# Four graph layers on one core: who writes the three parts of the weighted one-hots

## The chip, the cores and the metric

The kernel runs on one core of one Trainium2 chip. The metric is the device time of one execution in microseconds (us), lower is better. The engines are named as the profile names them: PE (TensorE; PEld its weight loads), DVE (VectorE), ACT (ScalarE), POOL (GpSimd) and SP, which only issues DMAs.

## What is computed

Four graph layers over N = 6250 nodes of 256 features and E = 106250 edges (100000 random ones, made symmetric, and a loop for each node), sorted by destination. Each layer is added to its input and normalized. Cut to what matters:

```
edge_index = stack([src, dst])
x = layernorm(x + L0(x))        # attention over rows of x picked by src and dst
x = layernorm(x + L1(x))        # out = segment_sum(h[src] * norm, dst),           h = x @ W
x = layernorm(x + L2(x))        # two GCN layers with edge weights and self loops:
                                #   out = segment_sum(dinv[row]*w*dinv[col] * h[row], col) + b, relu
x = layernorm(x + L3(x))        # out = segment_sum(vals * h[dst], src),           h = x @ W.T
```

So layers 1 and 2 (L2 holds two of them) sum the rows of a table h over the edges of each destination, and layer 3 sums over the edges the other way. The kernel calls the sum of layer 1 pass 1, the two of layer 2 passes 2 and 3, and the last one pass 4.

## The kernel before

The nodes are cut into NBK = 49 blocks of 128. The edges of a destination block fill NC = 18 chunks of 128 edges. In pass 1 a chunk is one gather of 128 rows (POOL, L2109, an indirect DMA into one of NG = 7 tiles G), a one-hot M of the destinations (DVE, L1287, NM = 4 tiles), and one matmul (PE, L2008) that adds M times the gathered rows to the block's sum. ACT writes the edge's weight into a last column of G (L1621).

Behind pass 1, in the same loop over its 882 chunks, runs the build of adjacency matrices for later passes. For the blocks of BORDER, one for every PITCH = 17 chunks, the edges are sorted into cells by pairs of blocks (cellhot, pick, pack, place on DVE; totals, rank, permute on PE; L1346 to L1380 and L1889 to L1907). Then ACT copies the cells' contents from PSUM, step "cells": the low part of the source ids to clf, everything in 16 bits to clb, and, for a dense block, the third part of the weights to clw in 32 bits (L1665 to L1668). A block has NPOS = 26 positions, two to a batch (CB = 2), so NBT = 13 batches. For each batch:

- DVE, step "pairhot": doh, one-hots of destinations, 128 x 256 in 16 bits (L1392), two of soh, one-hots of sources (L1394), and in a dense block the weighted one-hots wdoh, parts 0 and 1 (L1398).
- ACT, step "third": part 2 of wdoh, by one ACTIVATE for each of the two positions (L1676), with the weight as its scale. It waits for doh.
- PE, step "pair": doh times soh into PSUM (L1919). PE, step "weigh", dense blocks alone: soh times each of the three parts of wdoh, 6 matmuls for each position (L1931). It waits for wdoh of DVE (`s_v`) and of ACT (`s_tw`), and then for a free PSUM bank.
- ACT, steps "keep" and "keepw": the finished PSUM banks to atf or atp (L1685, L1688) and to awp (L1695). SP stores them from there (AT and AW).

A weight is the sum of three 16-bit parts, so that the matmuls in 16 bits give it in full. The last NDW = 22 blocks (numbers from NBW = 27 on) are dense: they have weighted matrices too, which passes 2 and 3 then load in place of gathers (L1967). BORDER spreads the 22 dense among the 27 sparse ones, so that mostly one follows the other. The tiles doh, soh and wdoh have NB = 4 buffers; DVE takes one again when PE's pairs and weighs of the batch four before are done. The PSUM banks of the build are a ring of three.

The order on each engine is fixed in the program. `build_steps` gives each step a due chunk: for a batch that starts at `at_`, pairhot at `at_`, third at `at_ + 1`, pair at `at_ + 1`, weigh at `at_ + 2`, keep at `at_ + 2`, keepw at `at_ + 3`, and 26 positions are spread over 17 chunks. An engine runs, for each chunk, first what the pass itself needs, then the steps that are due, in order, and waits where it has to. `chunks_of` is 882 for pass 1, 29 and 27 blocks' worth for passes 2 and 3.

Of the kernel before, what the change touches and what calls it, by code (L numbers as in the profile page):

```python
# [10 lines left out]
ALU = mybir.AluOpType  # L11
# [4 lines left out]
P = 128  # L16
# [16 lines left out]
CB, NB = 2, 4  # L33
# [600 lines left out]
def program(nc, a, out):  # L634
# [6 lines left out]
    with ExitStack() as ctx:  # L641
# [100 lines left out]
        slots = sb("slots", [P, NBK, NC])  # L742
        clb = [sb(f"clb{i}", [P, 5, NPOS], BF16) for i in range(2)]
        clf = [sb(f"clf{i}", [P, NPOS]) for i in range(2)]
        clw = [sb(f"clw{i}", [P, NPOS]) for i in range(2)]
        payw = sb("payw", [P, NDW, 3, NC], BF16)
        wrest = sb("wrest", [P, NDW, NC])
        cell = sb("cell", [P, NBK, NC], BF16)
# [185 lines left out]
        def vector(e):  # L934
# [3 lines left out]
            def done(ins, name=None):  # L938
                ins.then_inc(s_v, 1)
                n[0] += 1  # L940
                if name is not None:
                    at[name] = n[0]
                return n[0]
# [370 lines left out]
            def behind_(step):  # L1314
# [20 lines left out]
                elif kind == "cellhot":  # L1335
                    O_ = OH[j]
                    if i == 0:
                        w.wait_ge(s_ct, NPR + 2)
                        w.wait_ge(s_io, 7)
                        w.wait_ge(s_ev, project_of(1, NBK - 1) + 1)  # L1340
                        after("dsum", "d1")
                    if i >= 2:
                        w.wait_ge(s_rk, i - 1)
                        after(("load", i - 2))
                    w.wait_ge(s_du, i + 1)
                    done(e.tensor_tensor(twos(O_[:, :, :]), twos(celltab[:, own, :].unsqueeze(1).to_broadcast([P, NC, NPOS])),  # L1346
                                         celld[j][:, :, :].unsqueeze(2).to_broadcast([P, NC, NPOS // 2, 2]), ALU.is_equal), ("cellhot", i))
                elif kind == "pick":
                    w.wait_ge(s_rk, i + 1)
                    if i:  # L1350
                        after(("pack", i - 1))
                    done(e.tensor_tensor(sel[:, :, :], PR[:, 0:NPOS * NC].rearrange("p (c t) -> p c t", t=NPOS), OH[j][:, :, :],
                                         ALU.mult), ("pick", i))
                elif kind == "pack":
                    after(("pick", i))
                    if i:
                        after(("slots", i - 1))
                    done(e.tensor_reduce(slot0[:, :], sel[:, :, :], AX.X, ALU.add), ("pack", i))
                elif kind == "over":
                    after(("pack", i))  # L1360
                    done(e.scalar_tensor_tensor(out=OH[j][:, :, own + 1], in0=slot0[:, :], scalar=127.5, in1=OH[j][:, :, own],
                                                op0=ALU.is_ge, op1=ALU.mult), ("over", i))
                elif kind == "less":
                    after(("over", i))
                    done(e.tensor_tensor(OH[j][:, :, own], OH[j][:, :, own], OH[j][:, :, own + 1], ALU.subtract), ("less", i))
                elif kind == "slots":
                    done(e.scalar_tensor_tensor(out=slots[:, b, :], in0=OH[j][:, :, own + 1], scalar=-128.0, in1=slot0[:, :],
                                                op0=ALU.mult, op1=ALU.add), ("slots", i))
                elif kind == "load":
                    after(("less", i))  # L1370
                    w.wait_ge(s_pm, NC * i)
                    q_ = 5 if b >= NBW else 2
                    for q in range(q_):
                        done(e.tensor_tensor(twos(OHP[:, :, q, :]), payd[j][:, :, q, :].unsqueeze(2).to_broadcast([P, NC, NPOS // 2, 2]),
                                             twos(OH[j][:, :, :]), ALU.mult), ("load", i))
                elif kind == "place":
                    c = step[2]
                    after(("slots", i))
                    w.wait_ge(s_pm, NC * (i - 1) + c + 1)
                    done(e.tensor_scalar(S[:, c, :], iob[:, 0:P], slots[:, b, c:c + 1], None, ALU.is_equal), ("place", i, c))  # L1380
                elif kind == "pairhot":
                    n_ = NBT * i + step[2]
                    j0 = CB * step[2]
                    g = min(CB, NPOS - j0)
                    value = lambda q, m_: clb[j][:, q, j0:j0 + g].unsqueeze(1).to_broadcast([P, m_, g])
                    w.wait_ge(s_ce, i + 1)
                    if n_ >= NB:
                        before = n_ - NB
                        w.wait_ge(s_pc, batch_end(before))
                        if BORDER[before // NBT] >= NBW:  # L1390
                            w.wait_ge(s_wg, batch_end(before) - NPOS * (before // NBT - weighed_before(before // NBT)))
                    done(e.tensor_tensor(doh[n_ % NB][:, :, 0:g], irepD[:, :, 0:g], value(1, P), ALU.is_equal), ("doh", n_))  # L1392
                    for q in range(g):
                        done(e.tensor_scalar(soh[n_ % NB][:, q, :], iob[:, :], clf[j][:, j0 + q:j0 + q + 1], None, ALU.is_equal),  # L1394
                             ("pairhot", n_))
                    if b >= NBW:
                        after(("doh", n_))
                        done(e.tensor_tensor(wdoh[n_ % NB][:, 0:2, :, 0:g], doh[n_ % NB][:, :, 0:g].unsqueeze(1).to_broadcast([P, 2, P, g]),  # L1398
                                             clb[j][:, 2:4, j0:j0 + g].unsqueeze(2).to_broadcast([P, 2, P, g]), ALU.mult), ("weighted", n_))
                elif kind == "bad":  # L1400
                    after(("place", NBK - 1, NC - 1))
                    done(e.tensor_scalar(slots[:, :, :], slots[:, :, :], 127.5, 0.0, ALU.is_ge, ALU.add, accum_out=bad[:, :]), "bad")
                elif kind == "pad":

                    built(w)
                    w.wait_ge(s_bad, 1)
                    done(e.memset(keyS[96:128, ETAIL:EC], 8192), "pad")
                elif kind == "split":
                    w.wait_ge(L["src"], 3 * 16)
                    after("pad")  # L1410
                    done(e.tensor_scalar(tS[0][:, :], keyS[:, :], 7, None, ALU.logical_shift_right), "kS0")
                    done(e.tensor_scalar(tS[1][:, :], keyS[:, :], 127, None, ALU.bitwise_and), "kS1")
                    after("kS0")
                    done(e.tensor_copy(hi[:, :], tS[0][:, :]))
                    after("kS1")
                    done(e.tensor_copy(lof[:, :], tS[1][:, :]), "keysS")
                elif kind == "deg":
                    if b == 0:
                        w.wait_ge(s_io, 9)
                        after("keysS")  # L1420
                    if b < NDEG:
                        degrees(b)
                elif kind == "dinv" and b == 0:
                    w.wait_ge(s_dgs, NDEG)
                    done(e.tensor_scalar(degS[:, :], PR[:, 0:NBK], 1.0, None, ALU.add), "degS")
                elif kind == "dinv" and b == 1:
                    w.wait_ge(s_sq3, 1)
                    for i in range(4):
                        newton("d3n", i, d3[:, :], degS[:, :], [t_[:, :] for t_ in rs])
                    at["d3"] = at["d3n", 3]  # L1430
                else:
                    w.wait_ge(s_bad, 1)
                    done(e.tensor_scalar(ok[:, 1:2], PC[:, 0:1], 0.5, None, ALU.is_lt), "ok1")
                    after("ok1")
                    done(e.tensor_tensor(ok[:, 0:1], ok[:, 0:1], ok[:, 1:2], ALU.mult), "ok")
                    after("ok")
                    done(e.tensor_copy(flag[:, :], ok[0:1, 0:1]), "flag")
# [76 lines left out]
        def scalar(e):  # L1514
# [126 lines left out]
            def behind_(step):  # L1641
# [16 lines left out]
                elif step[0] == "cells":  # L1658
# [5 lines left out]
                        w.wait_ge(s_v, max(at["pairhot", n_], at.get(("weighted", n_), 0)))  # L1664
                    e.copy(clf[i % 2][:, :], PC[:, 0:NPOS])  # L1665
                    if q_ == 5:
                        e.copy(clw[i % 2][:, :], PC[:, 4 * NPOS:5 * NPOS])
                    e.copy(clb[i % 2][:, 0:q_, :].rearrange("p k t -> p (k t)"), PC[:, 0:q_ * NPOS]).then_inc(s_ce, 1)  # L1668
                elif step[0] == "third":

# [2 lines left out]
                    w.wait_ge(s_ce, i + 1)  # L1673
                    w.wait_ge(s_v, at["doh", n_])
                    for q in range(min(CB, NPOS - j0)):
                        ins = e.activation(wdoh[n_ % NB][:, 2, :, q], doh[n_ % NB][:, :, q], ACT.Copy, scale=clw[i % 2][:, j0 + q:j0 + q + 1])  # L1676
                    ins.then_inc(s_tw, 1)
                elif step[0] == "keep":
                    i, m_ = step[1], step[2]
# [614 lines left out]
```

## Time and profile before

| | us |
|---|---|
| median of 3 runs | 3351.84 |
| lowest and highest | 3343.08, 3353.5 |
| the profiled execution | 3345.05 |
| its span, first to last instruction | 3343.2 |
| PE, DVE, ACT, POOL busy | 3084.6, 2304.2, 1742.7, 2036.7 |
| mean granted clock of PE | 0.976 of full speed |

A busy time is the time in which the engine has at least one instruction running; matmuls overlap, and so do ACT's instructions where they follow each other closely. So counts times mean durations can be more than the busy time. An engine's share of the span is a mean over stages that have different limits; for a change that lies in one stage the windows of that stage are the view to read, cut by what its loop repeats.

### The profile page before, as it was taken

The page shows a single profiled execution, that of the slowest core. Times are in us where ns is not written, and L with a number is a line of the kernel's source. Part 1 is how long each engine was busy: PE and PEld are TensorE (multiplying, and loading weights), DVE is VectorE, ACT ScalarE, POOL GpSimd, SP SyncE. Part 2 cuts the span into 40 slices and gives each one's busy share as a digit, 9 for nine tenths or more (in the row PEclk, how much of TensorE's full clock was granted, in tenths as well). Part 3 has the DMA queues.
Part 4 walks back from the last instruction along what each step waited for, and adds up shares of the span by engine and source line. Part 5 has one row for each costly group of instructions (what it writes and reads, how often), then busy time and mean ns, then how long its engine had stood idle before and what let it go on. Part 6 is the DMA issues. An engine that isn't in the chain of part 4 may idle for free.

```text
span 3343.2 us, 58417 instructions
## 1 busy us (share of the span) xinstructions
PE 3084.6 (92%) x18262; PEld 2501.9 (75%) x18262; DVE 2304.2 (69%) x9060; ACT 1742.7 (52%) x4775; POOL 2036.7 (61%) x2042
## 2 busy tenths in 40 slices
PE   6788988989988989799999999799999998999999
PEld 5665667757766667578888888688888886888887
DVE  6657988998899889567777777566666664323333
ACT  3555767767767767534444444344444453323232
POOL 6627777777777777677777777577777771000000
PEclk9899999999999999999999999899999999999999
DMA  6246878878778878666666666776667666444443
GB/s 199 76 178 193 255 233 257 253 236 256 248 240 261 253 227 257 216 195 204 206 202 204 204 200 199 238 217 211 214 208 216 210 201 226 151 142 147 167 167 117
DMA packets 335271, 692.18 MB, mean 207 GB/s; under 512 B 63028, under 2 KB 180496, under 8 KB 334062
## 3 DMA queue, kind: packets, MB, share of 16 engines
q1 hardware_dynamic: 237134, 424.16, 37.5%
q0 software_dynamic: 95888, 262.38, 27.4%
q8 instruction: 151, 2.47, 0.3%
q10 hardware_dynamic: 1936, 1.84, 0.2%
q14 instruction: 162, 1.33, 0.1%
HBM read 497.33 MB, written 190.82 MB: 206 GB/s over the span
## 4 chain that ended last, share of the span: by engine, by line
PE 68%; DVE 16%; DMA 7%; POOL 3%; ACT 3%; issue 2%; SPq 0%; DVEq 0%; ACTq 0%
PE PS L1967 25%; PE PS L2039 15%; PE PS L2010 6%; PE PS L2008 6%; DMA G<-T,idx 5%; DVE soh L1394 4%; PE PS L1931 3%; PE PS L1790 3%; DVE M L1287 2%; PE PS L1791 2%; DVE S L1380 2%; PE PS L1948 2%; DVE doh L1392 2%; POOL G L2109 2%; PE PS L1919 2%
## 5 line engine op out<-in xcount | busy, mean ns | idle before, releaser
L2109 POOL DMA_INDIRECT G<-T,idx x1890 | 1913.8, 1013 | 643.3 <-issue 267.5
L1967 PE MATMUL PS<-H,aw 128*128 128x256 f32 x4116 | 1053.0, 381 | 0.4 <-DMA aw<-AW 0.4
L1631 ACT ACTIVATE R<-G,wD 128x256 fp32r<-128x256 f32 x1008 | 509.5, 508 | 699.8 <-PE PS L2010 506.6
L1967 PEld LDWEIGHTS PS<-H,aw 128*128 128x128 f32 x4116 | 771.9, 191 | 111.9 <-DMA aw<-AW 0.8
L1296 DVE SCALAR_TENSOR_TENSOR R<-G,wD,R 128x256 fp32r<-128x256 f32 x1008 | 488.2, 484 | 373.0 <-ACT R L1631 368.7
L2008 PE MATMUL PS<-G,M 128*128 128x257 f32 x1764 | 602.8, 426 | 141.8 <-DMA G<-T,idx 54.2
L2010 PE MATMUL PS<-R,Mr 128*128 128x512 f32 x1008 | 586.2, 583 | 29.8 <-DVE R L1296 28.1
L2039 PE MATMUL PS<-HH,cr 128*128 128x512 f32 x2205 | 501.5, 390 | 0.3 <-DVE cr L1472 0.2
L2039 PEld LDWEIGHTS PS<-HH,cr 128*128 128x128 f32 x2205 | 413.5, 188 | 88.1 <-DVE cr L1472 2.6
L2008 PEld LDWEIGHTS PS<-G,M 128*128 128x128 f32 x1764 | 279.0, 196 | 214.7 <-DVE soh L1394 39.6
L1688 ACT CAST atp<-PS 128x512 bf16<-128x512 f32 x588 | 337.4, 574 | 195.1 <-PE PS L1919 182.1
L1394 DVE TENSOR_SCALAR soh<-iob,clf 128x256 bf16<-128x256 bf16 x1274 | 309.9, 293 | 0.0
L1732 ACT CAST cr<-br 128x3584 fp32r<-128x3584 bf16 (+1 forms) x42 | 125.0, 2976 | 348.5 <-PE PS L2039 299.3
L1289 DVE TENSOR_SCALAR Mr<-iot,dlo 128x128 fp32r<-128x128 f32 x1008 | 301.8, 300 | 0.0
L1472 DVE CAST cr<-br 128x3584 fp32r<-128x3584 bf16 (+1 forms) x42 | 81.1, 1931 | 319.9 <-PE PS L2039 225.9
L1931 PEld LDWEIGHTS PS<-wdoh,soh 128*128 128x128 bf16 x3432 | 229.6, 98 | 76.1 <-ACT wdoh L1676 16.1
L1287 DVE TENSOR_SCALAR M<-iot,dlo 128x128 f32<-128x128 f32 x882 | 251.2, 287 | 45.3 <-PE PS L2008 44.0
L1919 PE MATMUL PS<-soh,doh 128*128 128x256 bf16 x1225 | 275.2, 276 | 4.9 <-ACT awp L1695 2.6
L1931 PE MATMUL PS<-wdoh,soh 128*128 128x128 bf16 x3432 | 269.1, 221 | 6.7 <-ACT atp L1688 4.9
L2010 PEld LDWEIGHTS PS<-R,Mr 128*128 128x128 f32 x1008 | 193.4, 192 | 69.7 <-DVE R L1296 42.5
L1380 DVE TENSOR_SCALAR S<-iob,slots 128x128 bf16<-128x128 bf16 x882 | 213.5, 262 | 0.0
L1676 ACT ACTIVATE wdoh<-doh,clw 128x128 bf16<-128x128 bf16 x572 | 212.4, 445 | 0.1
(241 smaller groups left out, 3784.2 us busy)
## 6 DMA issues: line engine op xcount, KB each, us to landing
aw<-AW SPq DMA_DIRECT2D x294, 448.0 KB, 3.6
AT<-atp SPq DMA_DIRECT2D x539, 128.0 KB
br<-AT SPq DMA_DIRECT2D x77, 896.0 KB, 4.8
AW<-awp SPq DMA_DIRECT2D x264, 256.0 KB
G<-T,idx POOLq DMA_INDIRECT x1890
AT<-atf SPq DMA_DIRECT2D x49, 256.0 KB
T<-H SPq DMA_DIRECT2D x96, 128.0 KB
cr<-AT SPq DMA_DIRECT2D x7, 1024.0 KB, 5.2
```

The costliest lines, as they stand in the source:

```text
L1287: ins = e.tensor_scalar(M[m % NM][:, :], iot[:, :], dlo[:, b, c:c + 1], None, ALU.is_equal)
L1296: done(e.scalar_tensor_tensor(out=both[:, D:2 * D], in0=G[slot][:, 0:D], scalar=wD[:, b, c:c + 1], in1=both[:, 0:D].bitcast(F32), op0=ALU. ...
L1394: done(e.tensor_scalar(soh[n_ % NB][:, q, :], iob[:, :], clf[j][:, j0 + q:j0 + q + 1], None, ALU.is_equal), ("pairhot", n_))
L1631: e.activation(R[m % NR][:, 0:D], G[slot][:, 0:D], ACT.Copy, scale=wD[:, k // NC, k % NC:k % NC + 1]).then_inc(s_rw, 1)
L1688: e.copy(atp[n_ % 4][:, 0:wid], fill_bank(*step)[:, 0:wid]).then_inc(s_ar, 1)
L1919: ins = e.matmul(ps, d_, s_, start=j != own + 1, stop=True)
L1931: ins = e.matmul(ps[:, h * P:(h + 1) * P], soh[n_ % NB][:, q, h * P:(h + 1) * P], wdoh[n_ % NB][:, t, :, q], start=j != own + 1 and h == 0 ...
L1967: ins = e.matmul(ps, aw[n_ % NAW][:, s_ % 7, :], H[:, s_, :], start=s_ == 0, stop=s_ == NBK - 1)
L2008: e.matmul(ps, M[m % NM][:, :], G[slot][:, 0:D + 1], start=c == 0, stop=c == NC - 1).then_inc(s_mm, 1)
L2010: e.matmul(ps, Mr[m % NM][:, :], R[m % NR][:, :], start=c == 0, stop=c == NC - 1).then_inc(s_mm, 1)
L2039: ins = e.matmul(SET[g % 2][s % 4][:, :], cr[(j + 1) % 2][:, bb, (s % 4) * P:(s % 4 + 1) * P], HH[:, :, b, :], start=b == 0, stop=b == NBK ...
L2109: e.indirect_dma_start(G[slot][:, 0:D], None, TAB[p][0:N, :], bass.IndirectOffsetOnAxis(ap=idx[:, k // NC, k % NC:k % NC + 1], axis=0)).th ...
```

## The change

Of the three parts of wdoh DVE now writes only part 0, with one TENSOR_TENSOR over 256 elements in place of one over 512. ACT writes parts 1 and 2, with four ACTIVATEs for each batch in place of two. For the scales of both parts clw is twice as wide, and ACT's copy into it takes 52 columns of PSUM in place of 26. Nothing moves in the order of steps; waits and semaphores stay as they are. Beside that, the program is made with 8192 bytes of each SBUF partition reserved for the descriptors of POOL's DMAs, where it had the default of 16384.

```diff
--- before.py
+++ after.py
@@ -742,7 +742,7 @@
         slots = sb("slots", [P, NBK, NC])
         clb = [sb(f"clb{i}", [P, 5, NPOS], BF16) for i in range(2)]
         clf = [sb(f"clf{i}", [P, NPOS]) for i in range(2)]
-        clw = [sb(f"clw{i}", [P, NPOS]) for i in range(2)]
+        clw = [sb(f"clw{i}", [P, 2, NPOS]) for i in range(2)]
         payw = sb("payw", [P, NDW, 3, NC], BF16)
         wrest = sb("wrest", [P, NDW, NC])
         cell = sb("cell", [P, NBK, NC], BF16)
@@ -1395,8 +1395,7 @@
                              ("pairhot", n_))
                     if b >= NBW:
                         after(("doh", n_))
-                        done(e.tensor_tensor(wdoh[n_ % NB][:, 0:2, :, 0:g], doh[n_ % NB][:, :, 0:g].unsqueeze(1).to_broadcast([P, 2, P, g]),
-                                             clb[j][:, 2:4, j0:j0 + g].unsqueeze(2).to_broadcast([P, 2, P, g]), ALU.mult), ("weighted", n_))
+                        done(e.tensor_tensor(wdoh[n_ % NB][:, 0, :, 0:g], doh[n_ % NB][:, :, 0:g], value(2, P), ALU.mult), ("weighted", n_))
                 elif kind == "bad":
                     after(("place", NBK - 1, NC - 1))
                     done(e.tensor_scalar(slots[:, :, :], slots[:, :, :], 127.5, 0.0, ALU.is_ge, ALU.add, accum_out=bad[:, :]), "bad")
@@ -1664,7 +1663,7 @@
                         w.wait_ge(s_v, max(at["pairhot", n_], at.get(("weighted", n_), 0)))
                     e.copy(clf[i % 2][:, :], PC[:, 0:NPOS])
                     if q_ == 5:
-                        e.copy(clw[i % 2][:, :], PC[:, 4 * NPOS:5 * NPOS])
+                        e.copy(clw[i % 2][:, :, :].rearrange("p k t -> p (k t)"), PC[:, 3 * NPOS:5 * NPOS])
                     e.copy(clb[i % 2][:, 0:q_, :].rearrange("p k t -> p (k t)"), PC[:, 0:q_ * NPOS]).then_inc(s_ce, 1)
                 elif step[0] == "third":
 
@@ -1673,7 +1672,9 @@
                     w.wait_ge(s_ce, i + 1)
                     w.wait_ge(s_v, at["doh", n_])
                     for q in range(min(CB, NPOS - j0)):
-                        ins = e.activation(wdoh[n_ % NB][:, 2, :, q], doh[n_ % NB][:, :, q], ACT.Copy, scale=clw[i % 2][:, j0 + q:j0 + q + 1])
+                        for t in range(2):
+                            ins = e.activation(wdoh[n_ % NB][:, 1 + t, :, q], doh[n_ % NB][:, :, q], ACT.Copy,
+                                               scale=clw[i % 2][:, t, j0 + q:j0 + q + 1])
                     ins.then_inc(s_tw, 1)
                 elif step[0] == "keep":
                     i, m_ = step[1], step[2]
@@ -2281,7 +2282,7 @@
     import numpy as np
     import concourse.bacc as bacc
     from concourse.bass_utils import run_bass_kernel_spmd as run
-    nc = bacc.Bacc("TRN2", target_bir_lowering=False, num_devices=1)
+    nc = bacc.Bacc("TRN2", target_bir_lowering=False, num_devices=1, dynamic_dma_scratch_size=8192)
     arrays, args = {}, {}
     for name, v in inputs.items():
         v = np.ascontiguousarray(v)
```

## Rows read from the trace of the kernel before

**Rows 1.** The page: busy us of each engine, then the group of gathers.

```profile
PE 3084.6 (92%) x18262; PEld 2501.9 (75%) x18262; DVE 2304.2 (69%) x9060; ACT 1742.7 (52%) x4775; POOL 2036.7 (61%) x2042
...
L2109 POOL DMA_INDIRECT G<-T,idx x1890 | 1913.8, 1013 | 643.3 <-issue 267.5
```

**Rows 2.** Windows, three stages: busy us (xinstructions), granted clock, DMA share, GB/s.

```profile
core 0: us, PE busy (x) PEld busy (x) DVE busy (x) ACT busy (x) POOL busy (x), PEclk, DMA share, GB/s
280.00:1390.00 1110.00, 981.20 (x8063) 745.17 (x8063) 993.91 (x4877) 815.79 (x2832) 850.16 (x831) 0.98 0.79 248
1390.00:2240.00 850.00, 813.92 (x4153) 681.15 (x4152) 583.22 (x1960) 364.01 (x792) 626.22 (x619) 0.98 0.66 205
2240.00:3343.00 1103.00, 1080.52 (x4842) 906.75 (x4840) 556.19 (x1680) 430.78 (x735) 401.60 (x405) 0.99 0.56 184
```

**Rows 3.** Windows, the 22 dense blocks, doh to doh: first, last, sum.

```profile
296.45:324.00 27.55, 24.39 (x238) 19.63 (x239) 23.67 (x111) 22.02 (x76) 21.15 (x21) 1.00 0.78 248
...
1345.01:1371.28 26.27, 21.13 (x206) 17.19 (x207) 19.97 (x96) 20.56 (x67) 20.48 (x20) 1.00 0.76 238
sum 581.58, PE 526.94 PEld 420.69 DVE 510.00 ACT 480.44 POOL 447.03; mean PE 23.95 PEld 19.12 DVE 23.18 ACT 21.84 POOL 20.32
```

**Rows 4.** Windows, the 21 sparse blocks behind a dense one: first, last, sum.

```profile
324.00:343.47 19.47, 17.64 (x122) 12.42 (x120) 18.01 (x95) 13.94 (x50) 14.88 (x16) 1.00 0.85 265
...
1326.70:1345.01 18.31, 16.55 (x119) 12.17 (x119) 17.56 (x95) 12.14 (x46) 14.04 (x15) 1.00 0.82 257
sum 407.11, PE 358.67 PEld 259.86 DVE 381.18 ACT 272.53 POOL 310.99; mean PE 17.08 PEld 12.37 DVE 18.15 ACT 12.98 POOL 14.81
```

**Rows 5.** Windows, 22 dense blocks, first to last L1676: first, two others, sum.

```profile
300.61:325.55 24.94, 22.68 (x229) 18.34 (x229) 21.32 (x101) 21.45 (x74) 19.14 (x20) 1.00 0.83 264
...
847.85:872.76 24.91, 24.91 (x232) 20.33 (x232) 20.12 (x91) 21.66 (x75) 18.51 (x18) 0.90 0.79 256
...
1004.65:1028.37 23.72, 22.78 (x228) 18.26 (x228) 22.37 (x108) 21.76 (x75) 18.22 (x19) 1.00 0.83 265
...
sum 551.03, PE 510.36 PEld 410.62 DVE 480.03 ACT 477.51 POOL 422.84; mean PE 23.20 PEld 18.66 DVE 21.82 ACT 21.70 POOL 19.22
```

**Rows 6.** Waits in 280:1390: who waited for whom, us, times, longest.

```profile
ACT atp L1688 <- PE PS L1919: 180.2, 219, 4.4
...
ACT awp L1695 <- PE PS L1931: 43.7, 75, 3.1
...
PE PS L2008 <- DMA G<-T,idx: 33.3, 50, 2.3
DVE doh L1392 <- PE PS L1931: 31.0, 34, 3.5
...
PEld PS L1931 <- ACT wdoh L1676: 16.1, 45, 0.7
...
DVE doh L1392 <- PE PS L1919: 7.2, 13, 1.1
```

**Rows 7.** Groups on DVE in 280:1390: count, busy us, mean ns, idle.

```profile
L1392 DVE TENSOR_TENSOR doh<-irepD,clb 128x256 bf16<-128x256 bf16 x635 | 179.3, 282 | 40.2 <-PE PS L1931 31.0 <-PE PS L1919 7.2 <-issue 0.6
L1398 DVE TENSOR_TENSOR wdoh<-doh,clb 128x512 bf16<-128x512 bf16 x286 | 118.2, 413 | 0.0
```

**Rows 8.** Groups on ACT in 280:1390.

```profile
L1676 ACT ACTIVATE wdoh<-doh,clw 128x128 bf16<-128x128 bf16 x572 | 212.4, 445 | 0.1
...
L1668 ACT CAST clb<-PS 128x130 bf16<-128x130 f32 x22 | 6.4, 292 | 0.0
...
L1667 ACT COPY clw<-PS 128x26 f32<-128x26 f32 x22 | 4.3, 195 | 0.0
```

**Rows 9.** Timeline of ACT: start us, us, instruction.

```profile
1009.78 0.74 ACT L1676 ACTIVATE wdoh<-doh,clw 128x128 bf16<-128x128 bf16 x2
1010.38 0.18 ACT L1621 COPY G<-wD 128x1 f32<-128x1 f32 x1
```

**Rows 10.** Tile G: the gathers, ns min/median/max.

```profile
L2109 POOL DMA_INDIRECT G<-T,idx x1890: 940/948/2497, 229.9 to 2778.1; - x189
```

## The prediction

> **What bounds the kernel now.** I read four things, in this order. First the page's busy times and the three stages: TensorE (PE) is busy for 92% of the span, and the edit's instructions all lie in the stage of pass 1, 280 to 1390 us [rows 1, 2]. In that stage PE is busy for 981 of 1110 us, VectorE (DVE) for 994, ScalarE (ACT) for 816 and GpSimd (POOL) for 850. So nobody is full on average, and the stage has to be cut by block. The 22 dense blocks (the ones with weighted one-hots) lie between sparse ones, so I cut from the first doh of a block to the first doh of the next: a dense block takes 581.58/22 = 26.4 us, with PE at 23.95, DVE at 23.2 and ACT at 21.84 us busy [rows 3]. A sparse block behind a dense one takes 407.11/21 = 19.4 us with PE 17.1, DVE 18.15, ACT 13.0 [rows 4]. In a sparse block DVE is the fullest, at 94%; in a dense one PE and DVE go nearly together (91% and 88%), ACT follows at 83%.
>
> Last, the part that decides: from the first L1676 of a dense block to its last, that is while ACT has this work at all. These windows take 551.03/22 = 25.05 us and ACT is busy for 21.70 of them, so 3.34 us are idle; in the tightest one it is busy for 21.76 of 23.72, in another for 21.66 of 24.91, where PE is busy throughout at a granted clock of 0.90 [rows 5]. What is idle there is mostly ACT waiting for PE to finish the pairs that it then copies out [rows 6]. PE waits for ACT's one-hots only 45 times, 16.1 us in all [rows 6]: today they arrive in time.
>
> **DVE's part.** It now writes two of the three parts with one TENSOR_TENSOR of 512 elements, 286 of them at 413 ns. What is left is one part, 256 elements with the same kind of operands as doh on L1392, at 282 ns [rows 7]. That saves 131 ns in each, 1.7 us in a dense block, 37 us in all. I take the row as it stands: same operation, shape, type and strides. Halving the elements saves only a third of the time, since most of an instruction isn't elements. Below nothing I don't go, for the remaining work is a half of the old one.
>
> **ACT's part.** A third is now two ACTIVATEs for each batch (572 in all), and becomes four. The mean duration is 445 ns [rows 8], but the price on ACT isn't that: two of them, started at 1009.78, let the next instruction start at 1010.38 [rows 9]. A pair takes 0.60 us of the engine, one 0.30, the rest lies under its neighbour. So the added pair costs 0.60 us in each batch, 13 x 0.60 = 7.8 us in a dense block, 22 x 7.8 = 172 us in all. The bounds of the price are 0.30 us (from row to row) and 0.445 us (the full duration, no overlap). I take 0.30, since the row is of the same instruction on the same tiles, back to back.
>
> The Trainium skill, "ScalarE: Activation LUTs", section "What ACT_TABLE_LOAD costs", says that back-to-back ACTIVATEs overlap by about 93 ns. The trace's overlap is larger, 0.445 - 0.30 = 0.145 us. By the page the added pair would be 2 x (0.445 - 0.093) = 0.70 us, 9.2 us in a dense block instead of 7.8, and the sum below would come out 22 x 1.35 = 30 us higher; the measured start times decide.
>
> **Copies of the cells.** The copy into clw grows from 26 to 52 columns. The rows bound it: 26 columns to fp32 take 195 ns, 130 columns to bf16 292 ns [rows 8], so the growth is under 0.1 us, once in a dense block, under 2 us in all. I take 1 us, and leave it out of the sum as smaller than what I round.
>
> **The smaller scratch.** The diff also halves the bytes reserved for the descriptors of POOL's DMAs, for the whole kernel. No row of before shows an operation that waits for them: 1890 gathers take 940/948/2497 ns (least, median, most), with a mean of 1013 [rows 1, 10]. At worst what is above the median, (1013 - 948) x 1890 = 123 us of POOL, would double; at best nothing happens. POOL is busy for 77% of pass 1 and less later, and PE's wait for gathers is 33.3 us [rows 2, 6], so the visible part would be at most about as large again. I take zero: at most seven gathers are in flight, whichever size is set.
>
> **The sum.** In the windows of rows 5 ACT's work grows from 21.70 to 29.5 us, and the window is only 25.05 now. PE needs 23.2 and DVE 21.8 - 1.7 = 20.1 of it. So ACT becomes the one that sets a dense block. If it never idled, the window would be 29.5; it idles for 1.96 us today in its tightest window [rows 5], part of which the added work fills too, while some of its waits for PE at the start of a block remain. I take 1.3 us, two thirds of that, so 30.8, a growth of 5.75, say 5.8 us. The saving on DVE is then hidden behind ACT and brings nothing in a dense block.
>
> A part comes back in the sparse block behind it. DVE and POOL now reach the ends of their buffers seldom (DVE waits for PE to free a one-hot in 34 + 13 of 637 batches [rows 6]); with PE held up by ACT they will stand there at the end of each dense block, some one chunk further ahead than today. A chunk is 19.4/17 = 1.1 us, and a sparse block can't become shorter than PE's 17.1 us. I take 1.0 us, with 0 and 2.3 (19.4 - 17.1) as ends. ACT itself can't hand much of its load to the sparse block: a weighted one-hot must be there before PE's weigh of the same batch, and everything behind it on PE, the next pairs, permutes and gathers' matmuls, waits in order with it.
>
> Net 4.8 us for each of 22 dense blocks: 22 x 4.8 = 105.6 us. Against the profiled execution (3345.05 us, 3343.2 its span) that makes 3450.7 us; the median of the three runs lies 6.8 us above that execution, and the runs are 10 us apart, so I add half: about 3455 us.
>
> **Ends of the range.** Low: ACT's idle time is used up wholly (7.8 - 3.34 = 4.5) and the sparse block gives back all 2.3, so 22 x 2.2 = 48 us: 3396, rounded 3400. High: none of the 7.8 finds idle time and nothing comes back, 172 us: 3520. More than 172 isn't possible at 0.30 us each, since a chain of waits can pass each added instruction once.
>
> **Rivals.**
> - *ACT's load is levelled out, and DVE's relief shows* (faster). Over a dense and a sparse block ACT has 21.84 + 12.98 = 34.8 us in 45.8; with 7.8 more it is 42.6, still under it. If ACT could run ahead through the four buffers of doh and wdoh into the slack of the sparse blocks, DVE (88% to 94% full) would be the bound and its 37 us would be gained: 3315. It decides from the point where at least 7.8 us of idle time can be reached from a dense block, where its own windows have 3.34. Against it: four buffers are four batches of 13, and the work can't begin before that block's cells are copied. 0.04. Half-way between this and the forecast, within 0.3%: 0.03.
> - *The added ACTIVATEs don't overlap* and cost 0.445 us each: 26 x 0.445 = 11.6 us in a block, less the 2.0 of idle and 1.0 of recovery as above, 8.6 x 22 = 189 us: 3540. For it: two pairs that write columns of two parts in turn are a new order. Against: the start times of [rows 9]. 0.05.
> - *The scratch shows*: gathers are held up in all passes. By the bound above up to 33 us beside the ACT's term in pass 1, and up to 123 - 33 = 90 where POOL's excess falls on PE in passes 2 and 3: 3455 to 3580. 0.03.
> - *The edit on DVE does less than it says*, the smaller TENSOR_TENSOR staying near 413 ns. By the forecast DVE isn't what ends a dense block, so the time stays at 3455; it lies inside the forecast.
>
> **Chances.** The forecast (ACT sets the dense blocks, 3400 to 3520) has 0.85, the rivals as given. A measurement of this kernel tells about 0.3% (10 us) from no change. Faster by more: 0.04; within: 0.03; slower: 0.93. The range 3400 to 3520 leaves out 0.15.
>
> **What the profile after should show.** The window from first to last of the ACTIVATEs of a dense block: about 31 us with ACT busy for 95% or more; their mean near 445 ns with start to start at 0.30. TENSOR_TENSOR into wdoh: 286 at about 280 ns. PE's wait for wdoh from ACT, 16 us now, becomes the largest of its waits in pass 1, over 60 us. DVE waits for a free one-hot in far more than 47 batches. ACT's wait for pairs, 180 us now, falls by some 40 us. Sparse blocks behind dense ones: 18 to 19 us. Stages 1390 to 2240 and 2240 to 3343: lengths unchanged within 0.5%. Wrong it would be if ACT's idle time in those windows stays near 3 us (then the growth is nearer to 7.8), if sparse blocks shorten by over 2 us, or if passes 2 and 3 change.

## The result, and the profile after

The changed kernel takes 3412.0 us (median of 4 runs, 3406.98 to 3420.45) against 3350.0 us before; the ratio is 1.0186, 95% interval 1.0169 to 1.0204, so 62 us slower. Its profiled execution took 3409.3 us with a span of 3407.4, against 3345.05 and 3343.2. The forecast was 3455 us in a range of 3400 to 3520.

First, where the time is. Tile G in both kernels: the matmul that ends pass 1 is the last of 1764 (ns min/median/max, then the first and the last start in us). Before, then after:

```profile
L2008 PE MATMUL PS<-G,M x1764: 377/381/796, 232.8 to 1410.2; 128*128 128x257 f32 x196
```

```profile
L2110 POOL DMA_INDIRECT G<-T,idx x1890: 943/949/2710, 228.8 to 2842.7; - x189
...
L2009 PE MATMUL PS<-G,M x1764: 380/380/795, 231.8 to 1475.5; 128*128 128x257 f32 x196
```

Pass 1 ends at 1475.5 us in place of 1410.2, 65.3 us later. From there to the end of the span it is 3407.4 - 1475.5 = 1931.9 us, before 3343.2 - 1410.2 = 1933.0: passes 2 to 4 didn't change. The gathers themselves are as they were (median 949 ns, before 948 [rows 10]).

The page's busy line, ACT's and DVE's groups in pass 1 (count, busy us, mean ns, idle before), and four ACTIVATEs of one batch with what follows them (start us, us):

```profile
PE 3104.3 (91%) x18262; PEld 2489.3 (73%) x18262; DVE 2275.6 (67%) x9060; ACT 1904.4 (56%) x5347; POOL 2025.1 (59%) x2042
...
L1676 ACT ACTIVATE wdoh<-doh,clw 128x128 bf16<-128x128 bf16 x1144 | 378.7, 439 | 0.1
...
L1398 DVE TENSOR_TENSOR wdoh<-doh,clb 128x256 bf16<-128x256 bf16 x286 | 80.5, 281 | 0.0
```

```profile
1056.60 1.32 ACT L1676 ACTIVATE wdoh<-doh,clw 128x128 bf16<-128x128 bf16 x4
1057.78 0.20 ACT L1589 ACTIVATE rq<-q 128x2 f32<-128x2 f32 x1
```

Both edits cost what the rows of before said. DVE's TENSOR_TENSOR went from 413 to 281 ns (forecast 282 [rows 7]), and four ACTIVATEs, from 1056.60 to the next instruction at 1057.78, take 1.18 us of ACT (forecast 1.20 [rows 9]). ACT is busy for 1904 us, 162 more than in [rows 1], where 172 were forecast.

The windows from the first to the last of these ACTIVATEs in a dense block (first, the slowest, a tight one, and the sum of all 22; columns as in [rows 2]):

```profile
core 0: us, PE busy (x) PEld busy (x) DVE busy (x) ACT busy (x) POOL busy (x), PEclk, DMA share, GB/s
299.90:328.71 28.81, 24.57 (x234) 18.36 (x233) 21.37 (x108) 28.54 (x100) 22.27 (x22) 1.00 0.80 249
...
835.09:866.88 31.79, 25.81 (x234) 19.63 (x233) 23.40 (x117) 28.99 (x101) 21.01 (x21) 0.95 0.70 217
...
933.94:963.07 29.13, 24.27 (x234) 18.41 (x233) 20.15 (x101) 28.88 (x101) 20.15 (x22) 1.00 0.78 246
...
sum 652.69, PE 541.58 PEld 406.33 DVE 486.02 ACT 634.03 POOL 455.46; mean PE 24.62 PEld 18.47 DVE 22.09 ACT 28.82 POOL 20.70
```

In [rows 5] they were 551.03 us, 25.05 each, with ACT busy for 21.70. Now they are 652.69 us, 29.67 each, with ACT busy for 28.82, which is 97%; in the tight one it is busy for 28.88 of 29.13. PE is busy for only 24.6 and DVE for 22.1. ACT is what ends a dense block. The waits in pass 1 (280 to 1452 us) say the same from the other side:

```profile
POOL G L2110 <- PE PS L2009: 171.2, 297, 2.7
...
ACT atp L1689 <- PE PS L1920: 141.7, 206, 2.9
PEld PS L1932 <- ACT wdoh L1676: 135.6, 195, 1.3
DVE doh L1392 <- PE PS L1932: 68.0, 65, 2.6
PE PS L1932 <- ACT wdoh L1676: 51.6, 123, 0.9
...
DVE doh L1392 <- PE PS L1920: 29.1, 32, 2.2
...
PE PS L2009 <- DMA G<-T,idx: 23.8, 34, 2.3
...
ACT awp L1696 <- PE PS L1932: 10.8, 20, 1.9
```

PE's wait for ACT's one-hots was 16.1 us for its weight loads [rows 6] and is 135.6; that of its matmuls is 51.6, and the two overlap in part, so they don't add up. DVE waits for a free buffer in 65 + 32 batches, before in 34 + 13. ACT's waits for PE fell from 180 to 142 us and from 44 to 11. And the largest is now POOL's: it waits for a matmul to free a tile of G, 171 us, before 88. It is the row that the explanation below turns on.

The windows grew by 652.69 - 551.03 = 101.7 us, pass 1 by 65.3. So 36 us came back outside of them, 1.7 us for each dense block.

### The profile page after: what moved, and what is told of

Same layout as the page of the kernel before. It is cut to its first block, busy times and chain, and to the rows that moved or that the text cites. A ratio compares the mean times of both kernels' runs of the same rounds, so it can differ in the third digit from the quotient of the medians.

```text
span 3407.4 us, 58989 instructions
## 1 busy us (share of the span) xinstructions
PE 3104.3 (91%) x18262; PEld 2489.3 (73%) x18262; DVE 2275.6 (67%) x9060; ACT 1904.4 (56%) x5347; POOL 2025.1 (59%) x2042
## 4 chain that ended last, share of the span: by engine, by line
PE 62%; ACT 13%; DVE 12%; DMA 6%; issue 4%; POOL 2%; SPq 0%; ACTq 0%; DVEq 0%
PE PS L1968 25%; PE PS L2040 14%; ACT wdoh L1676 7%; PE PS L2011 6%; DMA G<-T,idx 4%; PE PS L2009 4%; DVE soh L1394 3%; PE PS L1791 2%; PE PS L1792 2%; PE PS L1949 2%; ACT atp L1689 2%; ACT awp L1696 2%; DVE M L1287 2%; PE PS L1932 2%; DVE S L1380 2%
## 5 line engine op out<-in xcount | busy, mean ns | idle before, releaser
L2110 POOL DMA_INDIRECT G<-T,idx x1890 | 1902.4, 1007 | 721.4 <-issue 262.2
L1676 ACT ACTIVATE wdoh<-doh,clw 128x128 bf16<-128x128 bf16 x1144 | 378.7, 439 | 0.1
L1932 PEld LDWEIGHTS PS<-wdoh,soh 128*128 128x128 bf16 x3432 | 221.1, 97 | 189.7 <-ACT wdoh L1676 135.6
L1932 PE MATMUL PS<-wdoh,soh 128*128 128x128 bf16 x3432 | 278.3, 221 | 88.2 <-ACT wdoh L1676 51.6
L1394 DVE TENSOR_SCALAR soh<-iob,clf 128x256 bf16<-128x256 bf16 x1274 | 317.3, 299 | 0.1
L1392 DVE TENSOR_TENSOR doh<-irepD,clb 128x256 bf16<-128x256 bf16 x637 | 180.8, 284 | 102.8 <-PE PS L1932 68.0
```

Of the source, the lines that this page charges most:

```text
L1676: ins = e.activation(wdoh[n_ % NB][:, 1 + t, :, q], doh[n_ % NB][:, :, q], ACT.Copy, scale=clw[i % 2][:, t, j0 + q:j0 + q + 1])
L1932: ins = e.matmul(ps[:, h * P:(h + 1) * P], soh[n_ % NB][:, q, h * P:(h + 1) * P], wdoh[n_ % NB][:, t, :, q], start=j != own + 1 and h == 0 ...
L2110: e.indirect_dma_start(G[slot][:, 0:D], None, TAB[p][0:N, :], bass.IndirectOffsetOnAxis(ap=idx[:, k // NC, k % NC:k % NC + 1], axis=0)).th ...
```

## The experiments

Each time is beside runs of the kernel before on the same chip. All the kernels below have the smaller scratch of the diff, since their tiles need its room; the first one tests that alone.

**The scratch alone.**

```diff
-    nc = bacc.Bacc("TRN2", target_bir_lowering=False, num_devices=1)
+    nc = bacc.Bacc("TRN2", target_bir_lowering=False, num_devices=1, dynamic_dma_scratch_size=8192)
```

> The kernel before with the smaller descriptor scratch of the diff and nothing else. If the scratch plays no part, as I take it: ratio 1.000 within 0.3%, the gathers' durations as before (median 948 ns). If the scratch carries part of the 62 us: up to 1.018, with more gathers above 1.6 us and PE waiting for gathers for more than 33 us.

Measured: 3351.8 us, ratio 0.9988 (0.9973 to 1.0003). The scratch costs nothing here. That rival is out.

**ACT's part alone.**

```diff
-        wdoh = [sb(f"wdoh{i}", [P, 3, P, CB], BF16) for i in range(NB)]
+        wdoh = [sb(f"wdoh{i}", [P, 4, P, CB], BF16) for i in range(NB)]
...
-                        ins = e.activation(wdoh[n_ % NB][:, 2, :, q], ...)
+                        for t in range(2):
+                            ins = e.activation(wdoh[n_ % NB][:, min(2 + t, 3), :, q], ...)
```

> ACT's part alone: DVE writes two parts as before, ACT writes part 2 and, beside it, two more one-hots for each batch into a fourth part that nobody reads. Theory (ACT sets the dense blocks, DVE's saving is hidden): same as the changed kernel within 0.3%, 55 to 75 us above before. Rival (the saving on DVE does reach the end, and the 62 us are a larger loss less a gain): 85 to 100 us above before.

Measured: 3419.3 us, ratio 1.0183 (1.0162 to 1.0204), 61 us. That is the changed kernel's 1.0186. DVE does its old work here, 38 us more than in the changed kernel, and the time is the same: DVE's saving is hidden behind ACT.

**Half the dose, and twice the dose.** As above, with `for t in range(2 - q)` (one ACTIVATE more for each batch) and with five parts and `for t in range(3)` (four more).

> As act_plus2, but with one more ACTIVATE for each batch, not two. Theory (idle time of ACT is filled first): ACT's work grows by 13 x 0.30 = 3.9 us in a dense block, of which some 2.5 us find idle time; the rest is mostly given back in the sparse block: 0 to 15 us above before. Rival (each ACTIVATE lies on the path at a fixed share, 62/572 = 0.11 us): 31 us above before.

> As act_plus2, with four more ACTIVATEs for each batch than before (two further parts that nobody reads). Theory: once ACT has no idle time left in a dense block, each further pair costs its whole 0.60 us: 22 x 7.6 = 167 us above act_plus2's 61, less a little more recovery in the sparse blocks, so 200 to 228 us above before. Rival (a fixed share for each ACTIVATE, as from before to act_plus2): 122 us above before.

Measured: one more, 3361.9 us, ratio 1.0024 (1.0009 to 1.0038), 8 us. Four more, 3566.4 us, ratio 1.0673 (1.0650 to 1.0696), 225 us. A fixed share for each ACTIVATE (31 and 122 us) is out by a factor of four and of two; it is free at first and then costs its whole time. The sums of the 22 windows with one, two and four more:

```profile
sum 593.07, PE 528.62 PEld 409.65 DVE 502.55 ACT 555.31 POOL 455.98; mean PE 24.03 PEld 18.62 DVE 22.84 ACT 25.24 POOL 20.73
...
sum 654.38, PE 544.46 PEld 409.09 DVE 519.84 ACT 634.57 POOL 465.61; mean PE 24.75 PEld 18.59 DVE 23.63 ACT 28.84 POOL 21.16
...
sum 811.37, PE 564.23 PEld 412.12 DVE 533.71 ACT 799.44 POOL 478.19; mean PE 25.65 PEld 18.73 DVE 24.26 ACT 36.34 POOL 21.74
```

| ACTIVATEs added for each batch | ACT busy in a window | its length | growth of all windows | growth of the kernel | what came back |
|---|---|---|---|---|---|
| 0 [rows 5] | 21.70 | 25.05 | | | |
| 1 | 25.24 | 26.96 | 42.0 | 8 | 34 |
| 2 | 28.84 | 29.74 | 103.4 | 61 | 42 |
| 4 | 36.34 | 36.88 | 260.3 | 225 | 35 |

The growth of the windows is from one profile each, that of the kernel from all runs. With the growth of pass 1 in the same profiles instead (its last matmul starts at 1423.1, 1479.0 and 1633.1 us, before at 1410.2) the last column is 29, 35 and 37.

That column is the surprise. The part that comes back is about the same, 29 to 42 us by either reckoning, whether the windows grow by 42 or by 260 us. It is no share of the loss but a stock that is filled once in each dense block and spent in the block behind it. Which stock?

**DVE's part alone, and the other way round.** DVE writes part 0 only, and PE reads it in place of the part left out; then DVE writes all three and ACT none.

```diff
 dve_half:
-   done(e.tensor_tensor(wdoh[n_ % NB][:, 0:2, :, 0:g], ..., ALU.mult), ("weighted", n_))
+   done(e.tensor_tensor(wdoh[n_ % NB][:, 0, :, 0:g], doh[n_ % NB][:, :, 0:g], value(2, P), ALU.mult), ("weighted", n_))
...
-   ... wdoh[n_ % NB][:, t, :, q],
+   ... wdoh[n_ % NB][:, (0, 0, 2)[t], :, q],
 dve_three:
-   done(e.tensor_tensor(wdoh[n_ % NB][:, 0:2, :, 0:g], ..., clb[j][:, 2:4, j0:j0 + g] ...
+   done(e.tensor_tensor(wdoh[n_ % NB][:, 0:3, :, 0:g], ..., clb[j][:, 2:5, j0:j0 + g] ...
-   S_.append((at_ + 1, ("third", i, j // CB)))
-   w.wait_ge(s_tw, weighed_before(i) * NBT + j // CB + 1)
```

> DVE's part of the change alone: DVE writes part 0 with 256 elements, ACT writes part 2 as before, and part 1 is left out (PE multiplies part 0 twice in its place, so its work is the same). DVE loses 286 x 0.132 = 38 us. If PE and ACT's copies share the bound in dense blocks: 0 to 15 us faster. If DVE were what sets dense blocks: 30 to 38 us faster (ratio 0.989 to 0.991).

> The other way round: DVE writes all three parts with one TENSOR_TENSOR of 768 elements, ACT none, and PE waits for DVE alone. DVE gains 286 x 0.13 = 38 us of work, ACT loses 172. Theory (before, PE and DVE share the bound and ACT's load is below it): 10 to 25 us slower than before, the mirror of the 19 us that dve_half gained. Rival (ACT's copies behind its one-hots already hold back PE before the change): faster than before.

Measured: dve_half 3335.2 us, ratio 0.9943 (0.9923 to 0.9962), 19 us faster, a little over what I expected. dve_three 3370.5 us, ratio 1.0072 (1.0046 to 1.0097), 24 us slower, as expected, although ACT was rid of 172 us of work. I read both at first as PE and DVE sharing the bound. The gathers say something else (group of gathers in pass 1: count, busy us, mean ns, idle before). Before, dve_half and dve_three, each from 280 to 1390 us:

```profile
L2109 POOL DMA_INDIRECT G<-T,idx x831 | 851.7, 1025 | 260.1 <-issue 172.5 <-PE PS L2008 87.6
...
L2108 POOL DMA_INDIRECT G<-T,idx x836 | 851.8, 1019 | 259.3 <-issue 169.8 <-PE PS L2007 89.6
...
L2108 POOL DMA_INDIRECT G<-T,idx x803 | 864.9, 1077 | 246.2 <-issue 170.8 <-PE PS L2007 75.4
```

The mean gather takes 1025 ns before, 1019 with the least work on DVE and 1077 with the most, and POOL is idle for 246 to 260 us in each. Of that, 170 to 173 us have no releaser but POOL's own issue. A stretch of POOL in the kernel before, row by row:

```profile
1007.95 1.04 POOL L2109 DMA_INDIRECT G<-T,idx  x1 [0.30 <-issue]
1009.30 0.94 POOL L2109 DMA_INDIRECT G<-T,idx  x1 [0.31 <-issue]
1010.55 0.95 POOL L2109 DMA_INDIRECT G<-T,idx  x1 [0.32 <-issue]
1011.81 1.22 POOL L2109 DMA_INDIRECT G<-T,idx  x1 [0.30 <-PE PS L2008]
```

A gather starts about 0.30 us after the last one's end, every time, so a gather with its issue takes 1.25 us and more. Those 0.30 us aren't counted as busy, nor as anyone's wait. With them, POOL has 1025 + 300 = 1325 ns for each of 831 gathers, 1101 us of a stretch of 1110. **POOL is full in pass 1 of the kernel before**, where its busy share says 77%, and the pass is as long as its 882 gathers: counted over the whole pass, only 14 of the 881 gaps between them are longer than 0.35 us. No run changed POOL's own pace and nothing else, so this rests on the profiles. In dve_three it is full too (5 such gaps), with gathers that are 52 ns longer: 882 x 52 = 46 us at most. Its profiled execution was the slowest of four, 3381.7 us, 37 over that of before, and its pass 1 ended 36 us later; the 24 us are the median's. In dve_half the gathers are 6 ns shorter in this pair of profiles, 5 us, and its pass 1, from the first gather to the last matmul, is 7 us shorter; the two profiled executions differ by 10 us, the medians by more. So the rest of the 19 us isn't explained by this pair. But the mean gather was 1036 ns in scratch_only and 1040 in before_gathers9 below, also with before's work on DVE, so 6 to 21 ns shorter, or 5 to 19 us; that much the profiles of one kernel differ.

That DVE's instructions lengthen the gathers is what the Trainium skill, "SBUF — State Buffer", section "Who interferes with whom", would have: a DVE instruction with two inputs in SBUF contends with a GpSimd instruction that reads SBUF, and wdoh's TENSOR_TENSOR has two. The trace agrees for the three parts (1077 against 1025 ns). Within one trace it can be seen too: of the 882 gathers of pass 1 in dve_three, the 315 that overlap one of wdoh's TENSOR_TENSORs take 1180 ns in the mean, the others 1007; before, with 512 elements, 291 take 1054 and the others 1005; in dve_half, with 256, 281 take 1013 and the others 1018. So of the shortest ones, which have two inputs in SBUF as well, the trace shows no clear cost. How it comes about inside a gather no run here shows.

**A third that is due earlier.**

```diff
-                    S_.append((at_ + 1, ("third", i, j // CB)))
+                    S_.append((at_, ("third", i, j // CB)))
```

> The changed kernel with ACT's step third due one chunk earlier, at the chunk of its doh. Theory (ACT's throughput sets the dense blocks): nothing gained, within 0.3% of the changed kernel, since the sum of ACT's work is the same. Rival (PE waits because the one-hots are made too late in ACT's order, not because ACT is full): the 187 us that PE waits for ACT's one-hots fall and 20 to 60 us come back.

> The kernel before, with the smaller scratch and ACT's step third due one chunk earlier, as in after_third_early. If the 14 us gained there came from ACT's full load (an earlier start uses idle time at the head of a dense block), before, where ACT has idle time, gains nothing: within 0.3%. If PE's 16 us of waits for late one-hots count: up to 15 us faster.

Measured: on the changed kernel 3391.8 us, ratio to before 1.0142 (1.0121 to 1.0163), 47 us instead of 62; on the kernel before 3350.4 us, ratio 1.0007 (0.9995 to 1.0019). I had expected nothing for the first and missed; for the rival, which asked 20 to 60 us, the 15 that came back are too little. The sum of the windows is

```profile
sum 627.62, PE 513.06 PEld 407.96 DVE 477.92 ACT 619.69 POOL 449.58; mean PE 23.32 PEld 18.54 DVE 21.72 ACT 28.17 POOL 20.44
```

so 28.53 us for a dense block, ACT busy for 28.17. It is still full (99%), and the window is 1.1 us shorter. What moved is which of ACT's work lies in the window: its one-hots begin a chunk sooner, when ACT had idle time at the head of a dense block. Where ACT isn't the bound, the same edit is worth nothing. That this is the whole reason was argued from these windows, not tested by itself.

**Which buffers hold the stock.** Six one-hot buffers, and then nine tiles of gathered rows, on the changed kernel; nine tiles on the kernel before.

```diff
-CB, NB = 2, 4
+CB, NB = 2, 6
...
-NG, NM, NX = 7, 4, 4
+NG, NM, NX = 9, 4, 4
```

> The changed kernel with six buffers of doh, soh and wdoh in place of four. Theory (ACT is full from the first to the last third of a dense block, and DVE's waits for a free buffer cost nothing there): 0 to 15 us faster than the changed kernel, what DVE's longer lead gives the sparse block behind. Rival (the four buffers keep ACT from spreading its work into the sparse blocks): ACT has 26.8 + 15.3 = 42.1 us in a pair of blocks of 49.3, so with room enough up to 62 us come back.

> The changed kernel with nine tiles for gathered rows. My theory of the time that came back in sparse blocks is that PE, DVE and POOL do part of the next work inside the longer dense blocks, until their buffers are full. If POOL's seven tiles limit that: 10 to 25 us faster than the changed kernel. If not: within 0.3% of it.

> The kernel before, with the smaller scratch and nine tiles for gathered rows in place of seven. PE waits for gathers for 33 us in pass 1 of before, most of it in sparse blocks that follow a sparse one. If POOL's lead is what is short there: 5 to 25 us faster than before. If POOL's own pace (1.24 us for each gather) sets it: within 0.3%.

Measured: with six one-hot buffers 3411.3 us, ratio 1.0207 (1.0185 to 1.0228), nothing gained, where I had expected 0 to 15 us; pass 1 ends at 1476.9 us, without them at 1475.5. With nine tiles on the changed kernel 3370.7 us, ratio to before 1.0072 (1.0050 to 1.0095): 24 us over before in place of 62, so 38 us back, more than I expected. On the kernel before 3342.7 us, ratio 0.9984 (0.9971 to 0.9998), within 0.3%. So gathered rows are the stock, or most of it; other buffers, such as the four tiles M, weren't tried. The group of gathers of the changed kernel from 280 to 1452 us, then with nine tiles to 1410 us, and the sum of the windows with nine tiles:

```profile
L2110 POOL DMA_INDIRECT G<-T,idx x826 | 835.6, 1012 | 337.1 <-PE PS L2009 171.2 <-issue 165.9
...
L2110 POOL DMA_INDIRECT G<-T,idx x821 | 832.8, 1014 | 297.9 <-issue 164.6 <-PE PS L2009 133.3
```

```profile
sum 643.00, PE 540.13 PEld 399.08 DVE 497.98 ACT 632.52 POOL 475.00; mean PE 24.55 PEld 18.14 DVE 22.64 ACT 28.75 POOL 21.59
```

With seven tiles POOL waits 171 us for PE to free one (before 87.6 us in 265 times, a row shown further down, so 0.33 us each, little more than the ordinary 0.30 us before a gather); with nine 133 us. The windows changed little, 643.0 us against 652.7, which is 10 of the 38 us. They are 92 us longer than before, and 24 us remain, so 68 us come back outside them instead of 36 to 42. In a dense block POOL gathers ahead until its tiles are full; in the sparse block behind it the chunks go faster than 1.25 us each until that lead is spent. The gaps between gathers say the same: longer than 0.35 us are 14 of 881 before, 124 in the changed kernel, 192 in act_plus4 and 69 with nine tiles. Before, POOL seldom fills even seven tiles, and more of them give nothing.

The same can be read off the sparse blocks, if they are cut on ACT: from the end of the last L1676 of a dense block to the first of the next, with one sparse block in between (17 such stretches), it is 20.55 us in the mean before, 18.86 in the changed kernel, 18.93 with two and 18.93 with four ACTIVATEs added, and 17.99 with nine tiles.

**A try at a faster kernel.** The kernel before with nine tiles, the earlier third and five one-hot buffers.

> A try at a kernel faster than both: before with nine tiles for gathered rows, step third one chunk earlier and five buffers of one-hots. Expected 0 to 25 us faster than before, mostly by the gathers; nothing if PE and DVE's own work sets the blocks.

Measured: 3352.5 us, ratio 1.0015 (1.0004 to 1.0027). Nothing gained, as has to be where POOL's pace sets pass 1. In the profiled execution the gathers are even longer, 1055 ns in the mean from 280 to 1400 us, and pass 1 ends at 1425.0 us; which of the three edits does that, no run here shows. Of all kernels run, none that computes everything was faster than before by over 0.3%.

## Why the prediction was right, and where its steps were off

- **Sign and place: right.** The growth lies in pass 1's dense blocks; ACT is full there; DVE's saving is hidden (act_plus2); the scratch costs nothing (scratch_only); passes 2 to 4 are unchanged.
- **Prices: right.** 281 ns forecast as 282; 0.60 us for the added pair, measured 1.18 - 0.60 = 0.58. The rival of 0.445 us without overlap is out: act_plus4 against act_plus2 costs (225 - 61)/(22 x 26) = 0.29 us for each added ACTIVATE. By the 93 ns of overlap in the Trainium skill, "ScalarE: Activation LUTs", section "What ACT_TABLE_LOAD costs", it would have been 0.35 us, an estimate from the page and the 445 ns of [rows 8]; the runs don't agree with it.
- **ACT's idle time in a dense block: taken as 1.3 us, measured 0.85** (29.67 - 28.82), and ACT's busy time as 29.5, measured 28.8. Together a growth of 4.6 us in place of 5.8, 22 x 1.13 = 25 us of the miss.
- **What comes back behind a dense block: taken as 1.0 us, measured 1.7** (36 us in all, up to 42 in act_plus2), the other 14 us. The reason was half right: the ends of buffers. But I named DVE's as well as POOL's, and bounded it by PE's work in a sparse block (2.3 us). More one-hot buffers give nothing (after_deep), two more gather tiles give 38 us (after_gathers9). The two terms together make 39 of the 41 us between the sum's 105.6 and the 64.3 of the profiled executions.
- **"What bounds the kernel now" was wrong**, though it didn't carry the sign. I called PE (91%) and DVE (88%) the fullest in a dense block, DVE (94%) in a sparse one, and POOL 77% full. POOL paces pass 1. It was in [rows 6]'s own view, two lines that I left out, from 280 to 1390 us: POOL idle by its own issue, and by PE.

```profile
POOL G L2109 <- issue: 172.5, 566, 0.3
POOL G L2109 <- PE PS L2008: 87.6, 265, 1.7
```

- So the rival on the other side, ACT's load levelled out, had the wrong gain too: its 37 us on DVE are worth 19 (dve_half), by way of the gathers if at all. And more buffers don't level the load: ACT is 97% busy from first to last one-hot with four, 28.86 of 29.90 us with six. An earlier due chunk moved some of it (after_third_early).
- **The signs in the profile.** Right: PE's wait for one-hots over 60 us (135.6 for its weight loads), DVE's waits for buffers far over 47 (97), ACT's wait for pairs down by 40 (39), the windows with ACT over 95% (97%). Wrong: windows of 31 us (29.7). Unclear: sparse blocks behind dense ones of 18 to 19 us. Cut from doh to doh as in [rows 3, 4], dense and sparse blocks now sum to

```profile
sum 628.13, PE 524.22 PEld 396.11 DVE 479.22 ACT 589.73 POOL 452.23; mean PE 23.83 PEld 18.00 DVE 21.78 ACT 26.81 POOL 20.56
...
sum 434.87, PE 385.81 PEld 275.02 DVE 382.77 ACT 322.11 POOL 300.77; mean PE 18.37 PEld 13.10 DVE 18.23 ACT 15.34 POOL 14.32
```

that is 28.55 and 20.7 us: the sparse ones look longer. That is the cut. It follows DVE's doh, and DVE, one-hots ahead of the stalled PE, opens the next block before ACT and PE have left the dense one. Cut on ACT they are 1.7 us shorter, as shown above (20.55 and 18.86). A window has to be cut on the engine that is the bound.

## What to carry to other kernels

Moving work off an engine pays only if the engine that takes it has that much idle time in the same stretch; take the idle time from windows cut around the work itself, and price a run of instructions by start to start, not by mean duration. Count an engine's issue gaps as load before calling it free: GpSimd at 77% busy, with 0.30 us between gathers that nobody is to blame for, was the pace of the whole pass. What comes back after a stall is a stock limited by a buffer's depth, so it pays once for each stall, whatever the stall's length; two doses of the same cost tell it from a share.

## What the runs showed of the hardware

- POOL needs at least 0.94 us for a gather of 128 rows of 1 KB, and 0.30 us between two of them, 1.25 us each in the median, however free the tiles are.
- The mean gather was 1077 ns beside DVE's TENSOR_TENSORs of 768 elements, 1025 beside those of 512 (1036 and 1040 in two more profiles), 1019 beside those of 256. Those that overlap one took 1180, 1054 and 1013 ns, the others of the same traces 1007, 1005 and 1018.
- ACTIVATEs of 128 x 128 in 16 bits, 439 to 445 ns each in the mean, start 0.29 to 0.31 us apart when they follow each other, two or four in a row alike.
- Half the scratch for POOL's descriptors makes no difference with seven tiles of gathers (ratio 0.9988). With nine tiles only the halved scratch was run (0.9984 on the kernel before).
